# Second attention layer: scores on 32-row groups, input statistics one step ahead, closing rows written in place

## The reference

```python
def _mha(x, Wqkv, bqkv, Wo, bo):           # S=16, B=256, D=128, H=4, hd=32
    q, k, v = jnp.split(x @ Wqkv.T + bqkv, 3, axis=-1)      # to heads: (B, H, S, hd)
    scores = jnp.einsum('bhqd,bhkd->bhqk', q, k) * (1.0 / np.sqrt(hd))
    att = jax.nn.softmax(scores, axis=-1)
    o = jnp.einsum('bhqk,bhkd->bhqd', att, v)
    return o @ Wo.T + bo

y = _layer_norm(x + _mha(x, Wqkv, bqkv, Wo, bo), g1, be1)
z = _layer_norm(y + _moe(y, Wg, W1, b1, W2, b2), g2, be2)   # one of 8 experts for each token
x = x + _layernorm(z)                       # and x in front is layernorm of the first layer's output
```

## Time and profile before

| | us |
|---|---|
| median of 3 runs | 648.04 (647.04 to 653.3) |
| the profiled execution, whole run | 649.26 |
| its span, first to last instruction | 647.5 |

### The profile page before, as it was taken

How to read it: one execution, slowest core, us unless ns; L and a number is a source line. 1 busy time by engine, 2 the same in 40 slices (tenths; PEclk the granted TensorE clock), 3 DMA queues, 4 the chain that set the end, 5 groups by cost and what they waited for, 6 DMA issues and landing times. The chain is left out here.

```text
span 647.5 us, 16117 instructions
## 1 busy us (share of the span) xinstructions
PE 530.5 (82%) x5228; PEld 398.6 (62%) x5228; DVE 454.8 (70%) x1285; ACT 373.4 (58%) x989; POOL 327.1 (51%) x543
## 2 busy tenths in 40 slices
PE   2899999999999999999917888887766229999920
PEld 2576666666665566666506777776655229999920
DVE  2265789888888888888534888886786605788870
ACT  1215676676676576676604988866772015677750
POOL 5141134444456555421245367767888710377776
PEclk9999999999999999999956999979995559999975
DMA  4200523110000010010110000000000222234333
GB/s 107 72 2 2 164 68 53 23 23 17 19 15 9 18 20 19 19 19 19 36 32 32 2 1 2 2 3 9 17 23 29 73 60 67 45 49 63 35 33 33
DMA packets 38100, 21.63 MB, mean 33 GB/s; under 512 B 13433, under 2 KB 36353, under 8 KB 38018
## 3 DMA queue, kind: packets, MB, share of 16 engines
q1 hardware_dynamic: 18544, 10.65, 7.2%
q0 software_dynamic: 6640, 4.92, 5.4%
q10 hardware_dynamic: 12834, 5.04, 3.1%
HBM read 10.11 MB, written 8.12 MB: 28 GB/s over the span
## 5 line engine op out<-in xcount | busy, mean ns | idle before, releaser
L331 DVE TENSOR_REDUCE nmax<-psA 128x2 f32<-128x512 f32 x256 | 164.9, 686 | 62.3 <-PE psA L209 61.7
L493 ACT ACTIVATE pr<-psB 128x512 f32<-128x512 f32 x250 | 136.0, 595 | 93.7 <-PE psB L226 93.6
L209 PE MATMUL psA<-km,qp 24*128 24x256 f32 x768 | 127.9, 429 | 2.2 <-DVE nmax L331 1.7
L226 PE MATMUL psB<-q,km 26*128 26x256 f32 (+1 forms) x752 | 111.6, 413 | 0.4 <-DMA q<-mT 0.4
L209 PEld LDWEIGHTS psA<-km,qp 24*128 24x128 f32 x768 | 80.9, 199 | 34.7 <-DVE nmax L331 23.2
L1602 POOL DMA_INDIRECT out<-wz,ys x39 | 63.5, 1628 | 54.4 <-ACT wz L1557 45.6
L586 POOL TENSOR_TENSOR km<-kraw,rows_of 128x768 f32<-128x768 f32 x16 | 23.5, 1468 | 120.6 <-ACT kraw L468 113.0
L226 PEld LDWEIGHTS psB<-q,km 26*128 26x128 f32 (+1 forms) x752 | 69.7, 190 | 1.5 <-DMA q<-mT 0.8
L240 PE MATMUL psO<-pr,v 128*32 128x256 f32 x1024 | 69.3, 389 | 0.1
L1165 ACT ACTIVATE prob<-psS,nbias 128x128 f32<-128x128 f32 x128 | 45.6, 381 | 12.5 <-DVE nbias L984 12.4
L1458 DVE TENSOR_TENSOR hT<-psH,e_nb1T 128x512 f32<-128x512 f32 x39 | 27.0, 692 | 31.7 <-PE psH L1419 23.8
(11 more groups left out here) (198 smaller groups left out, 1173.6 us busy)
## 6 DMA issues: line engine op xcount, KB each, us to landing
q<-mT SPq DMA_DIRECT2D x256, 1.0 KB
ys<-y_sorted SPq DMA_DIRECT2D x39, 72.0 KB, 1.9
e_w<-W ACTq DMA_DIRECT2D x1, 2048.0 KB
e_w<-W ACTq DMA_DIRECT2D x4, 512.0 KB
xs<-x_all SPq DMA_DIRECT2D x16, 128.0 KB
out<-x_all SPq DMA_DIRECT2D x15, 128.0 KB, 3.7
x_all<-x SPq DMA_DIRECT2D x1, 1536.0 KB, 9.0
out<-wz,ys POOLq DMA_INDIRECT x39
```

The costliest lines, as they stand in the source:

```text
L209: last = T.matmul(psA[:, (16 * b + n) % 3, c * L1:(c + 1) * L1], query_part(b, h, depth, c), keys(b, h, depth, slice(0, L1)), start=True, ...
L226: last = T.matmul(bank_of(b, h)[:, c * L1:(c + 1) * L1], keys(b, h, depth, slice(c * P, (c + 1) * P)), queries(b, h, depth, slice(0, L1)), ...
L331: V.tensor_reduce(nmax[:, b % 2, hf, :, at], psA[:, (16 * b + n) % 3, :].rearrange("p (c m) -> p c m", c=2), AX.X, ALU.max, negate=True).t ...
L493: A.activation(pr[:, h % PRING, :, :].rearrange("p c l -> p (c l)"), bank_of(b, h), ACT.Exp, scale=SCALE1).then_inc(S["b_free"], 1)
```

## The change

- `qT2` loses its head axis: all of q goes into one array of 128 partitions by one ACT instruction, and k follows it on ACT too. The zeroing of qT2 on POOL and `q_zero` go.
- Scores: PE takes heads in two pairs. The product of head h reads only rows 32h to 32h+31 of qT2 and kT2. Bank psS[s] now holds the heads 2*pair + s, for both c, and the mask product covers two blocks at once (256 columns, four of them instead of eight). The mask tile is twice as wide. PE waits on a new semaphore `s_half` before the products of the second pair. `maxima` and `exponentials` run over s in place of c, and the products with 1/sum wait for all eight exponentials.
- DVE calls `norm_x(t + 1)` behind `apply_x(t)`, POOL calls `ready_x(t + 1)` at the end of its step, ahead of the sends.
- `finish_y` writes straight into y_all; yout, the copy and `y_kept` go, and with them its waits on `xy_full` and `y_kept`. PE transposes out of y_all, the sends wait on `y_ok`.

The diff, cut to its core:

```diff
-        mask = sb("mask", [P, P], BF16)
+        mask = sb("mask", [P, 2 * P], BF16)
...
-        qT2 = sb("qT2", [P, 2, H2, L1])
+        qT2 = sb("qT2", [P, 2, L1])
...
-                    for c in range(2):
-                        pe.wait_ge(S["p_ok"], count(8 * (i - 1) + 4 * c + 4))
-                        for h in range(H2):
-                            at = psS[c][:, h * P:(h + 1) * P]
-                            T.matmul(at, identh[:, :], mask[:, :], start=True, stop=False)
-                            last = T.matmul(at, qT2[:, n, h, c * P:(c + 1) * P],
-                                            kT2[:, n, c * P:(c + 1) * P], start=False, stop=True)
-                        last.then_inc(S["s_full"], 1)
+                    for pair in range(2):
+                        for s in range(2):
+                            if pair == 0:
+                                pe.wait_ge(S["p_ok"], count(8 * (i - 1) + 4 * s + 4))
+                            T.matmul(psS[s][:, 2 * pair * P:(2 * pair + 2) * P], identh[:, :], mask[:, :], start=True,
+                                     stop=False)
+                        if pair == 1:
+                            pe.wait_ge(S["s_half"], 2 * i + 2)
+                        for c in range(2):
+                            for s in range(2):
+                                h, u = 2 * pair + s, 2 * pair + c
+                                last = T.matmul(psS[s][:, u * P:(u + 1) * P],
+                                                qT2[C2 * h:C2 * h + C2, n, c * P:(c + 1) * P],
+                                                kT2[C2 * h:C2 * h + C2, n, c * P:(c + 1) * P], start=False,
+                                                stop=(c == 1))
+                                if c == 1:
+                                    last.then_inc(S["s_full" if pair else "s_half"], 1)
...
-                            last = T.transpose(psXY[:, (2 + c) * P:(3 + c) * P], yout[:, (m - 7) % 2, c, :],
+                            last = T.transpose(psXY[:, (2 + c) * P:(3 + c) * P], y_all[:, 2 * (t - 7) + c, 0:P],
                                                ident[:, :])
...
-                dve.wait_ge(S["xy_full"], t)
-                dve.wait_ge(S["y_kept"], count(i - 1))
-                V.tensor_tensor(yout[:, n, :, :], yg[:, :, :], rows[:, 2:3, :].broadcast_to([P, 2, P]),
+                V.tensor_tensor(y_all[:, 2 * i:2 * i + 2, 0:P], yg[:, :, :], rows[:, 2:3, :].broadcast_to([P, 2, P]),
                                 ALU.add).then_inc(S["y_ok"], 1)
...
             def iteration(t, m):
                 if t in SORT_AT:
                     mark(SORT_AT[t])
-                if has(t, 0):
-                    norm_x(t, m % 2)
-                if isinstance(t, int) and t == 0:
+                if t == 0:
+                    norm_x(0, 0)
                     make_mask()
-                if has(t, 1):
-                    dve.wait_ge(S["qk_full"], count(t))
-                    dve.wait_ge(S["s_full"], count(2 * (t - 1) - 2))
-                    V.tensor_scalar(kT2[:, (m - 1) % 2, :], psQK[:, L1:2 * L1], u_col[:, 1:2], None,
-                                    ALU.add).then_inc(S["k_ok"], 1)
                 if has(t, 0):
                     apply_x(t, m % 2)
+                if has(t + 1, 0):
+                    norm_x(t + 1, (m + 1) % 2)
...
-                if has(t, 7):
-                    i, n = t - 7, (m - 7) % 2
-                    dve.wait_ge(S["y_ok"], count(i + 1))
-                    dve.sem_inc(S["passed"])
-                    V.tensor_copy(y_all[:, bass.ds(i * 2, 2), 0:P], yout[:, n, :, :]).then_inc(S["y_kept"], 1)
...
-                    act.wait_ge(S["k_ok"], count(t))
-                    for h in range(H2):
-                        mine = slice(C2 * h, C2 * h + C2)
-                        last = A.activation(qT2[mine, (m - 1) % 2, h, :], psQK[mine, 0:L1], ACT.Identity,
-                                            bias=u_col[mine, 0:1])
-                    last.then_inc(S["q_ok"], 1)
+                    A.activation(qT2[:, (m - 1) % 2, :], psQK[:, 0:L1], ACT.Identity,
+                                 bias=u_col[:, 0:1]).then_inc(S["q_ok"], 1)
+                    A.activation(kT2[:, (m - 1) % 2, :], psQK[:, L1:2 * L1], ACT.Identity,
+                                 bias=u_col[:, 1:2]).then_inc(S["k_ok"], 1)
...
-                if has(t, 0):
-                    ready_x(t, m % 2)
-                if isinstance(t, int) and t == 0:
-                    G.memset(qT2[:, :, :, :], 0.0).then_inc(S["q_zero"], 1)
+                if t == 0:
+                    ready_x(0, 0)
...
                     if not late(t):
                         finish_y(i, n, t)
+                if has(t + 1, 0):
+                    ready_x(t + 1, (m + 1) % 2)
                 if t in SEND_AT:
                     send(*SEND_AT[t])
```

More of the change, by code:

```diff
@@ L813, in second_attention @@
                  "sums_full", "sums_read", "base_ok", "slots_ok", "pads_ok", "tail", "start_ok", "owner_ok", "rows_ok",
-                 "q_zero", "mask_ok", "xst", "xagg", "xstep", "xrs_ok", "xn2_ok", "xnb2_ok", "xy_full", "xy_read",
+                 "mask_ok", "s_half", "xst", "xagg", "xstep", "xrs_ok", "xn2_ok", "xnb2_ok", "xy_full", "xy_read",
                  "qk_full", "q_ok", "k_ok", "vo_full", "v2_ok", "r2_ok", "s_full", "m_step", "max_ok", "p_ok",
                  "rd_ok", "pn_ok", "pt_full", "pt_ok", "al_full", "att_ok", "lg_ok", "yst", "yagg", "ystep",
-                 "yln_step", "y_ok", "y_kept", "ids_ok"]
+                 "yln_step", "y_ok", "ids_ok"]
         S = {n: ctx.enter_context(nc.semaphore("l2_" + n)) for n in names}
@@ L1159, in _, with exponentials @@
             A.activation(wgT[:, :], psS[1][:, 0:NE], ACT.Copy).then_inc(S["wT_ok"], 1)
-            def exponentials(i, n, c):
-                act.wait_ge(S["max_ok"], count(2 * i + c + 1))
-                act.wait_ge(S["pt_full"], count(2 * (i - 2) + c + 1))
-                for h in range(H2):
-                    A.activation(prob[:, n, c, h, :], psS[c][:, h * P:(h + 1) * P], ACT.Exp,
-                                 bias=nbias[:, c, h:h + 1], scale=SCALE2,
+            def exponentials(i, n, s):
+                act.wait_ge(S["max_ok"], count(2 * i + s + 1))
+                act.wait_ge(S["pt_full"], count(2 * (i - 2) + 2))
+                for u in range(H2):
+                    h, c = u // 2 * 2 + s, u % 2
+                    A.activation(prob[:, n, c, h, :], psS[s][:, u * P:(u + 1) * P], ACT.Exp,
+                                 bias=nbias[:, s, u:u + 1], scale=SCALE2,
                                  accum_out=den[:, n, c, h:h + 1]).then_inc(S["p_ok"], 1)
@@ L1266, in send @@
                 pool.wait_ge(S["slots_ok"], k + 1)
-                pool.wait_ge(S["y_kept"], (lo + size) // 2)
+                pool.wait_ge(S["y_ok"], (lo + size) // 2)
                 for j in range(lo + first, lo + first + n):
@@ L1277, in finish_y @@
                 pool.wait_ge(S["yln_step"], 3 * i + 3)
-                pool.wait_ge(S["xy_full"], t)
-                pool.wait_ge(S["y_kept"], count(i - 1))
-                G.tensor_tensor(yout[:, n, :, :], yg[:, :, :], rows[:, 2:3, :].broadcast_to([P, 2, P]),
+                G.tensor_tensor(y_all[:, 2 * i:2 * i + 2, 0:P], yg[:, :, :], rows[:, 2:3, :].broadcast_to([P, 2, P]),
                                 ALU.add).then_inc(S["y_ok"], 1)
             def iteration(t, m):
-                if has(t, 0):
-                    ready_x(t, m % 2)
-                if isinstance(t, int) and t == 0:
-                    G.memset(qT2[:, :, :, :], 0.0).then_inc(S["q_zero"], 1)
+                if t == 0:
+                    ready_x(0, 0)
                 if has(t, 0):
```

19 lines of the change are left out of this document (8 added, 11 removed).

## The result

The changed kernel takes **632.28 us** (median of 4 runs, 630.56 to 633.14), the kernel before 649.25 us in the runs beside it (4 runs): a ratio of 0.9728, 95% interval 0.9673 to 0.9784. Its profiled execution took 633.14 us with a span of 631.4, 16.1 less than before.

The account below looks back on a forecast made before the run. A loop through several engines, with DVE and POOL waiting on each other, sets the step; POOL is late next. Savings 5.0 + 1.2 + 2.0 + 2.2 + 3.1 = 13.5 us from the median 648.04 give 634.5 us, range 628 to 641.

Parts of the forecast that it names:

- start, to x2n of step 6: Second attention's first steps: 1.26 us from dropping POOL's zeroing plus 3.8 from shorter ACT work, together 5.0 saved.
- steps 6 to 11: Even steps of the second attention: five steps from 8.24 to 8.0 us, set by POOL's loop, 1.2 saved.
- step 11: Sort step, x2n 11 to 12: 10.0 to 8.0 us as ready_x no longer waits for DVE's mark, 2.0 saved.
- step 12: Sort step, x2n 12 to 13: 10.7 to 8.5 us with DVE the bound, 2.2 saved.
- send steps: Steps 13 to 15, POOL full: two 0.72 waits go and collisions shrink, 3.1 us saved.
- 4 x 0.95: Steps 2 to 5, taken as set by ACT: two qT/kT rows replace four qT rows, 3.8 us saved.
- 0.80 + 0.18: Even steps: POOL's present collision loss with DVE's products, 0.80 us a step, plus 0.18 more after the change.
- rival 1: POOL's collisions with DVE's products dissolve: steps 6 to 12 at about 7.2 us, 629 in all; chance 0.20.
- Score block: PE's scores: 2.3 us a step against 2.67, worth nothing in even steps because POOL's loop covers it.
- 2 (the early steps don't follow ACT): Score block waits for all exponentials ahead of the transposes: only 1.3 of the start's 5.0 us, 638; chance 0.13.
- 3 (PE the longest loop): Scores take 4.0 us without overlap and with full drains, PE 8.5 a step: 642 us; chance 0.08.
- 4 (slower by PE's clock): PE falls to 1.2 GHz, 13.8 us a step; at five steps the time is 663 us; chance 0.05.

Follow-up runs that it names:

- ahead alone: Kernel before with only the statistics of x one step ahead (norm_x, ready_x): 638.82 us, ratio 0.9832.
- scores alone: Kernel before with only the new score block, one ACT row each for q and k, no zeroing: 645.64 us, ratio 0.9939.
- in place alone: Kernel before with only closing rows straight into y_all; yout, its copy and y_kept gone: 649.21 us, ratio 0.9975.
- the old scores in after: Kernel after with padded q in four ACT rows, zeroing and full-height products again, k still on ACT: 635.91 us, ratio 0.9793.
- the further orders: Kernel after with ready_x ahead of finish_y 629.70 us; finish_y on DVE in all steps 630.09, from step 13 631.71; early ready_x to step 9 plus latter 628.96.

## Why the prediction was right, and where it was off

634.5 was predicted, 632.28 came; the range of 628 to 641 holds it. The saving was forecast at 13.5 us and is 17.0 between the medians. By the terms of the sum, in us, from the two traces:

| term | predicted | measured |
|---|---|---|
| start, to x2n of step 6 | 5.0 | 8.5 |
| steps 6 to 11 | 1.2 | 2.0 |
| step 11 | 2.0 | 2.1 |
| step 12 | 2.2 | 2.0 |
| send steps | 3.1 | 3.2 |
| behind step 15 | 0 | 0.1 |
| second layer | 13.5 | 18.1 |
| first layer and experts | 0 | -1.9 |

The terms measured add to 17.9 by rounding. Of the -1.9, 1.8 is the later zero and 0.1 the experts; 18.06 less 1.93 is the span's 16.1.

**The mis-sized term is the start.** Of its 8.5 us, 2.8 lie ahead of x2n of step 2 and 5.7 behind it.

Ahead, the sum had the zeroing, 1.26; it is there (1.3 with the zeroing put back). What it left out is that x2n of step 1 stood behind kT on DVE, and kT waited for PE. The kernel before, DVE and PE, steps 1 and 2:

```profile
343.67 0.48 DVE L1056 TENSOR_SCALAR kT<-psQK,u_col 128x256 f32<-128x256 f32 x1 [2.54 <-PE psQK L865]
344.07 0.60 DVE L974 TENSOR_SCALAR x2n<-xs,nm_x,rs_x 128x128 f32<-128x128 f32 x2
...
346.62 2.07 PE L865 MATMUL psQK<-xy,uT 128*128 128x256 f32 x4 [1.16 <-ACT xy L1192]
```

With kT on ACT, x2n comes at 5.4 instead of 8.0: 1.3 us by the zeroing, 1.4 by the order. The prediction took kT off DVE's sum and did not ask who was queued behind its wait, which is the question it asked of each wait that the change adds.

Behind it, 4 x 0.95 was taken from ACT. From the last exponential of step 2 to that of step 6 it is 27.4 us before and 24.6 after: 0.70 a step, 2.8 in all. The size is near, but the step of the working behind it, that these steps follow ACT's work by itself, is not what the runs show. The same stretch takes 25.5 us with ahead alone, which leaves ACT's work as it was, and 28.5 with scores alone, which has the two short rows. Busy time from the last exponential of step 3 to that of step 5, in the order before, ahead alone, scores alone, after:

```profile
362.55:376.24 13.69, 11.68 (x117) 10.51 (x117) 11.98 (x35) 13.21 (x52) 3.00 (x8) 1.00 0.01 2
361.41:374.81 13.40, 11.69 (x118) 10.52 (x118) 10.23 (x32) 13.23 (x51) 5.04 (x7) 1.00 0.01 2
360.87:374.86 13.99, 12.13 (x116) 8.88 (x116) 11.08 (x33) 11.28 (x48) 2.95 (x8) 1.00 0.01 2
359.39:371.74 12.35, 11.51 (x118) 8.82 (x116) 10.30 (x32) 11.04 (x47) 2.98 (x6) 1.00 0.01 3
```

With ahead alone ACT is full (13.23 of 13.40). With scores alone it is not (11.28 of 13.99), and DVE waits for the scale from POOL, as it does in its even steps:

```profile
367.98 0.60 DVE L983 TENSOR_SCALAR x2n<-xs,nm_x,rs_x 128x128 f32<-128x128 f32 x2 [1.55 <-POOL rs_x L1255]
```

So two limits lay close together, and only both parts together give 12.35. The 3.8 us were credited to one part and need two; that 2.8 of them came is in part luck.

Another 0.6 is that x2n of step 6 now runs further ahead of that step's exponentials (7.4 us for 6.8). The other 2.4 us come in step 2 itself: from x2n to the first exponential it is 4.63 us before and 2.26 after. The first score block begins 1.2 us sooner against x2n, and takes 1.93 us (347.12 to 349.05) instead of 3.32 (349.34 to 352.66). In even steps the old block took 2.67, so of the 1.39 about 0.65 is the clock, by this estimate, and the rest the new shape. Busy time by stretch, before and then after:

```profile
336.00:344.80 8.80, 4.83 (x15) 3.40 (x16) 5.06 (x16) 1.57 (x5) 4.88 (x9) 0.50 0.00 0
344.80:350.60 5.80, 4.64 (x16) 3.73 (x17) 1.69 (x7) 3.24 (x8) 4.63 (x8) 0.50 0.22 89
```

```profile
337.80:344.80 7.00, 4.62 (x15) 3.46 (x16) 4.17 (x18) 1.64 (x5) 3.97 (x9) 0.50 0.00 0
344.80:348.15 3.35, 2.88 (x23) 2.19 (x22) 0.00 (x0) 1.74 (x5) 2.99 (x5) 0.99 0.18 73
```

Before, PE is granted half its speed (1.2 GHz) until 14.6 us behind zero; after, it has all of it (2.4 GHz) from 7.0 on. So the second QK and the first score block run at full speed: the second QK, kernel after,

```profile
345.71 1.13 PE L864 MATMUL psQK<-xy,uT 128*128 128x256 f32 x4 [0.47 <-ACT xy L1187]
```

takes 1.13 us instead of 2.07. Across the runs the early return goes with the new score part: the kernels with ahead alone, in place alone and the old scores in after had a second QK of 2.07 or 2.08 us and the full clock only at 14 to 15 us; in all nine traces with the new scores, the one with the zeroing back among them, it came between 7 and 10 us (the second QK takes 1.13 to 2.02 us in these nine). What brings it back is open. The shorter pause ahead of the second QK (0.47 us instead of 1.16) can't be it in five of the nine, after among them: there the clock rose at 6.7 to 7.8 us, ahead of that QK's start at 7.7 to 8.1, while PE had worked without a pause since 4.3. What the return is worth can be read a little: of the six traces with the same code up to x2n of step 6, the four with the clock back at 7.0 to 7.8 us have that x2n at 32.6 to 32.7, one with 9.3 has it at 32.9, and the one with 9.9 and a second low stretch at 34.0. The prediction looked at the clock only as a danger.

**Even steps.** The bound was named rightly: POOL's loop, with the 0.72 us until x2n left in it; that moving ready_x ahead shortens the step to 7.16 confirms it. 7.84 us came instead of 8.0. POOL's collisions cost 0.83 us a step and not 0.80 + 0.18: ve_y slips in ahead of the product (0.23), nm_y pays 0.56, and rs_y meets the second product and takes 1.22 instead of 0.71. In turn DVE's products are no longer stretched (0.69 both). The Trainium skill's page SBUF — State Buffer (Who interferes with whom) says that a tensor_tensor of DVE with both inputs in SBUF contends with GpSimd's reads, and calls the port pair that the two share an exclusive lock. The trace agrees: nm_y ends at 404.20, just behind the product's end at 404.12, and the maxima, which read psS, meet nothing. The dissolved collisions of rival 1 did not come.

**Score block.** 1.93 us with all four masks, as in step 2, for 2.3. Two errors cancel in part. The changes of form were priced too high: between the last product of the first pair and the first of the second stand two masks, two changes and the wait for s_half, and all of it is 0.32 us (402.12 to 402.44). The products were priced too low: 0.16 us each and not 0.11, so against 0.22 for the full height the row groups did not double the pace. If part of a change hides in the 0.16 can't be told. The block ends 1.24 us behind x2n (1.3 in the prediction) and DVE reaches the maxima at 3.01 (2.95), so the cover was worked out rightly. The block's price of nothing in even steps is shown by the kernel with the old scores. Its price at the start was not nothing.

**Steps with sorting and sends.** Step 11 at 7.88 (8.0 predicted), step 12 at 8.66 (8.5), the sends 3.2 (3.1). In steps 14 and 15 POOL no longer waits for x2n, and ve_y and nm_y take 0.24 and 0.22 us as predicted. Two small misses cancel: from add_bo to add_bo step 13 gives 0.3 us for 0.65, since its two sends take 0.45 longer, and step 15 gives 1.2 up to the end of its send for 0.9.

**Rivals.** The times of 2 (the early steps don't follow ACT) and 3 (PE the longest loop) fall by the table. What 2 says of ACT comes true where the statistics are not ahead, by another way than the one it named. 4 (slower by PE's clock): the granted clock was 1.00 in all even steps of after. It fell for a while in steps 2 to 5 (0.92 on average, the first row of the stretches) and in the send steps, where POOL sets the pace. The price that the prediction put on a step at 1.2 GHz, 13.8 us, is not borne out by the one even step that ran mostly there, in the kernel after without the part ahead; the step ahead of it and this one:

```profile
375.20:383.10 7.90, 6.41 (x59) 4.31 (x57) 6.12 (x19) 5.62 (x25) 6.25 (x11) 0.98 0.00 0
383.10:391.03 7.93, 7.93 (x54) 6.23 (x52) 6.15 (x19) 5.57 (x24) 6.24 (x11) 0.59 0.01 2
```

PE is busy all of its 7.93 us, and the step is not longer than its neighbour. What a longer stretch costs is open; this kernel's four runs with a mean granted clock of 0.877 to 0.887 took 648.3 to 651.1 us, its six with 0.896 to 0.910 took 643.2 to 645.7. Rival 1 has its word above.

## What to carry to other kernels

When an instruction is moved off an engine, ask what stood behind its wait, above all in the first steps, where nothing hides it; averages of the steady steps don't show that. A loop through two engines is shortened by what is taken out of that loop alone: a row of DVE in the shadow of a wait (kT), four rows of ACT with room and 0.7 us of PE gave nothing in the even steps and 5 us in the steps that fill the pipeline. Where two limits lie close together, as in steps 3 to 5, a part tried alone shows little of what it is worth beside the other. And once one bound is cut, look how far the next is: here DVE stood 0.7 us behind POOL, and the further orders won 0.7 to 3.3 us by the start of the experts, since what one engine gave the next took back.

## What the runs showed of the hardware

The first layer's time differs between executions of the same code. In thirteen traces the second layer's first statistics stand at 335.3 to 338.6 us. PE's granted clock shows where: the stretch of the first layer before and then after,

```profile
244.00:250.00 6.00, 6.00 (x70) 3.97 (x69) 5.31 (x14) 3.48 (x8) 4.63 (x10) 1.00 0.02 4
```

```profile
244.00:250.00 6.00, 6.00 (x58) 3.46 (x60) 4.50 (x12) 2.65 (x6) 4.58 (x10) 0.72 0.01 1
```

has 1.00 in one and 0.72 in the other, in a part that no edit touches and behind work of PE that fills the 6.00 us in both. The difference of zero is 1.8 us here. All thirteen traces go with it: behind the first 60 us, the three whose first layer has no short stretch at 0.50 have their zero at 335.3 to 335.9 us, the four with one at 336.0 to 337.5, the six with two at 337.8 to 338.6. What sets them off (chance, or the start's phase) stays open; for the comparison it means that about 2 us between two profiles of this kernel say nothing, and that the second layer has to be read from its own zero.

The other surprise is how early PE got its full clock back with the new score part, 7 to 10 us behind zero instead of 14 to 15. Why, and what the whole of it was worth against the kernel before, was not separated; 0.9 us of the second QK is the largest piece that the traces show by itself.
